# Fetching the rows of 5 of 416 table gathers on SyncE, row by row, in a DLRM interaction kernel on one Trainium2 core

## The reference

```python
e = stack([tbl_f[ids[:, f]] for f in range(26)], axis=1)        # (2048, 26, 64) float32 rows
x = layer_norm(dense @ Wd.T)                                     # (2048, 128)
y = layer_norm(einsum('bnd,ed->bne', e, Ws))                     # per row, 64 -> 128
y = layer_norm(einsum('bne,pn->bep', y, Wsi))                    # 26 rows mixed to 32
T = concatenate([x[:, None], swapaxes(y, 1, 2)], axis=1)         # (2048, 33, 128)
Z = einsum('bnd,bmd->bnm', T, T)[:, tril]                        # 528 products of pairs
z = layer_norm(Z @ Wl.T) * mask                                  # 512, 384 in use
h = relu(concat([z, dense]) @ W1 + b1); h = relu(h @ W2 + b2); out = h @ W3
```

## Time and profile before

| | |
|---|---|
| time, median of 3 runs | 577.3 us (575.38 to 578.61) |
| profiled execution, its own time | 577.42 us |
| its span, first to last instruction | 575.6 us |
| mean granted clock of TensorE | 0.976 |
| busy: PE / POOL / DVE / ACT | 505.9 / 400.8 / 397.2 / 293.6 us |
| first gather, start of the last one | 3.7 us, 528.7 us |

### The profile page before, as it was taken

How to read it: one execution, slowest core, us unless ns; L and a number is a source line. 1 busy time by engine, 2 the same in 40 slices (tenths; PEclk the granted TensorE clock), 3 DMA queues, 4 the chain that set the end, 5 groups by cost and what they waited for, 6 DMA issues and landing times.

```text
span 575.6 us, 18049 instructions
## 1 busy us (share of the span) xinstructions
PE 505.9 (88%) x7271; PEld 378.5 (66%) x7271; DVE 397.2 (69%) x707; ACT 293.6 (51%) x760; POOL 400.8 (70%) x422
## 2 busy tenths in 40 slices
PE   1969779999999898999989998988999899889975
PEld 1844457777776676777666766666676767668664
DVE  4787876777777767777676768766776777767800
ACT  1533565555554555545545646545454645555533
POOL 5777777777777777777777777777777777776000
PEclk9988799999999999899989999998999999999998
DMA  7711311313131312213131312213131211313020
GB/s 259 252 27 30 81 37 27 90 29 90 30 90 29 90 27 70 49 29 91 29 90 27 85 34 68 52 27 89 30 90 30 79 39 39 79 29 87 3 63 1
DMA packets 30999, 35.91 MB, mean 62 GB/s; under 512 B 10588, under 2 KB 19749, under 8 KB 30916
## 3 DMA queue, kind: packets, MB, share of 16 engines
q0 software_dynamic: 13408, 13.81, 12.5%
q1 hardware_dynamic: 17508, 20.94, 11.0%
HBM read 25.54 MB, written 9.18 MB: 60 GB/s over the span
## 4 chain that ended last, share of the span: by engine, by line
POOL 58%; issue 23%; PE 7%; DVE 5%; DMA 5%; ACT 2%; DVEq 0%; ACTq 0%
POOL rows L567 58%; DMA rows<-in_table,ids_based 5%; PE bank_z L700 2%; PE bank_z L633 1%; DVE scaled L397 1%; DVE scaled L372 1%; DVE y L407 1%; PE bank_aw L731 1%; DVE r_vec L433 1%; DVE bank_z L425 1%; ACT y_std L888 1%; PE bank_z L731 1%; PE bank_d L731 0%; DMA ids_based<-in_ids_based 0%; PE bank_z L681 0%
## 5 line engine op out<-in xcount | busy, mean ns | idle before, releaser
L567 POOL DMA_INDIRECT rows<-in_table,ids_based x416 | 399.4, 960 | 129.8 <-issue 122.0
L417 DVE TENSOR_REDUCE y_var<-y_sq 128x32 f32<-128x1024 f32 x63 | 76.9, 1220 | 41.3 <-ACT y_sq L882 41.1
L882 ACT ACTIVATE y_sq<-y 128x512 f32<-128x512 f32 x128 | 80.2, 631 | 34.2 <-DVE y L407 33.6
L433 DVE TENSOR_TENSOR r_vec<-y,bank_z 128x512 f32<-128x512 f32 x128 | 82.3, 684 | 2.4
L666 PE MATMUL bank_b<-mixed,gs_row 64*128 64x512 f32 x128 | 76.9, 682 | 7.8 <-ACT mixed L918 6.1
L681 PEld LDWEIGHTS bank_z<-r_vec 128*32 128x32 f32 x4096 | 46.0, 110 | 56.5 <-issue 54.7
L425 DVE RECIPROCAL bank_z<-y_std 128x32 f32<-128x32 f32 x63 | 22.8, 361 | 84.7 <-ACT y_std L888 84.7
L666 PE MATMUL bank_c<-mixed,gs_row 64*128 64x512 f32 x128 | 76.9, 682 | 0.0
L700 PE MATMUL bank_z<-wl,zd 128*128 128x512 f32 x160 | 75.2, 615 | 0.0
L639 PE MATMUL bank_z<-gram,rows_t 128*128 128x128 f32 x416 | 66.4, 300 | 8.7 <-ACT rows_t L903 8.7
L911 ACT ACTIVATE row_std<-row_var,eps 128x8 f32<-128x8 f32 (+1 forms) x64 | 19.2, 300 | 107.0 <-DVE row_var L381 97.7
(11 more groups left out here) (122 smaller groups left out, 633.8 us busy)
## 6 DMA issues: line engine op xcount, KB each, us to landing
zx<-zs SPq DMA_DIRECT2D x15, 560.0 KB, 3.6
rows<-in_table,ids_based POOLq DMA_INDIRECT x416
dense_t<-in_dense_t SPq DMA_DIRECT2D x1, 2048.0 KB, 9.1
wl<-in_wl SPq DMA_DIRECT2D x1, 1280.0 KB, 12.8
w<-in_w SPq DMA_DIRECT2D x1, 1280.0 KB
zd<-zx SPq DMA_DIRECT2D x15, 80.0 KB
zd<-zx SPq DMA_DIRECT2D x15, 70.0 KB
zd<-zx SPq DMA_DIRECT2D x16, 60.0 KB
```

Source lines behind the costliest of these rows:

```text
L417: v.tensor_reduce(y_var[:, k % BANKS, :], y_sq[:, k % 2, :, :].rearrange("e a (s p) -> e (a s) p", p=PROJ), AX_X, ALU.add).then_inc(y_var_ ...
L433: ins = v.tensor_tensor(r_vec[:, quad:quad + SPB // QUAD, :, Y0:PAD], y[:, k % 2, blk, :].rearrange("e (g s p) -> e g s p", g=SPB // QUAD, ...
L567: nc.gpsimd.indirect_dma_start(rows[t % 2][:, c, D * blk:D * (blk + 1)], None, io["table"], bass.IndirectOffsetOnAxis(ap=ids_all[:, n:n + ...
L882: nc.scalar.activation(y_sq[:, k % 2, blk, :], y[:, k % 2, blk, :], ACT.Square).then_inc(y_squared, 1)
```

## The change

Of the 26 gathers of tiles 3, 6, 9, 12 and 15 one is dropped, that of chunk 12, block 1, the last of its tile. Its 128 rows are fetched by SP with one DMA each, 640 in all. The row numbers lie in `own_ids`, on one partition: the ids and the first row of their table, which DVE adds up during the preparations. SP loads four row numbers at a time from there into registers, and issues four DMAs whose source address comes from them. It does 44 rows before its loop over the tiles, and then 44 in each turn of that loop: 4 between the store to `zx` and the wait for it, and 40 after the seven loads of `zd`. The buffer of rows is kept for four tiles in place of two, since SP writes to it long before POOL gets to that tile. POOL's wait on `rows_scaled` stays as it was.

```diff
+ROWS_KEPT = 4
+OWN_TILES = (3, 6, 9, 12, 15)
+OWN_CHUNK, OWN_BLK = CHUNKS - 1, 1
+OWN = P * len(OWN_TILES)
+OWN_FIRST, OWN_PART, OWN_BETWEEN = 44, 44, 4
+
+def gathers_of(t, q):
+    return [(c, blk) for c in GROUPS[q] for blk in range(2) if t not in OWN_TILES or (c, blk) != (OWN_CHUNK, OWN_BLK)]
...
-        rows = [sb(f"rows{i}", [P, CHUNKS, 2 * D]) for i in range(2)]
+        rows = [sb(f"rows{i}", [P, CHUNKS, 2 * D]) for i in range(ROWS_KEPT)]
+        own_ids = sb("own_ids", [1, 2, OWN], I32)
...
             add_row_base(1, TILES)
+            dve.wait_ge(s_own, 16)
+            v.tensor_tensor(own_ids[:, 1, :], own_ids[:, 1, :], own_ids[:, 0, :], ALU.add).then_inc(own_ready, 1)
...
             sp.dma_start(ids_based[:], io["ids_based"]).then_inc(s_ids, 16)
+            sp.dma_start(own_ids[:], io["own_ids"]).then_inc(s_own, 16)
...
+            def fetch(first, end):
+                end = min(end, OWN)
+                for at in range(first, end, 4):
+                    if at == 0:
+                        sp.wait_ge(own_ready, 1)
+                    if at % P == 0 and OWN_TILES[at // P] >= ROWS_KEPT:
+                        sp.wait_ge(rows_scaled, BANKS * (OWN_TILES[at // P] - ROWS_KEPT + 1))
+                    _, numbers = nc.values_load_multi_w_load_instructions(
+                        own_ids[0:1, 1, at:at + 4], engines=(mybir.EngineType.SP,), ...)
+                    for n in range(4):
+                        g, p = divmod(at + n, P)
+                        t = OWN_TILES[g]
+                        sp.dma_start(rows[t % ROWS_KEPT][p:p + 1, OWN_CHUNK, D * OWN_BLK:D * (OWN_BLK + 1)],
+                                     io["table"][bass.DynSlice(numbers[n], 1), :]).then_inc(own_landed[g], 16)
+
             sp.wait_ge(prep, prep_at["zd"])
+            fetch(0, OWN_FIRST)
             for t in range(TILES - 1):
                 sp.wait_ge(zs_kept, BANKS * (t + 1))
                 if t:
                     sp.wait_ge(z_moved, Z_MOVES * t)
                 sp.dma_start(zx.rearrange("j p k g i -> (j p) k g i"), zs[:]).then_inc(z_out, 16)
+                at = OWN_FIRST + OWN_PART * t
+                fetch(at, at + OWN_BETWEEN)
                 sp.wait_ge(z_out, Z_OUT * (t + 1))
                 if t:
                     sp.wait_ge(l_done, t)
                 for k in range(BLOCKS):
                     move_in(sp, k, z_moved)
+                fetch(at + OWN_BETWEEN, at + OWN_PART)
...
             def turn(k):
-                pe.wait_ge(gathered[t % 2][q], (t // 2 + 1) * (32 * len(GROUPS[q])))
+                pe.wait_ge(gathered[t % 2][q], 16 * sum(len(gathers_of(s, q)) for s in range(t % 2, t + 1, 2)))
+                if t in OWN_TILES and q == BANKS - 1:
+                    pe.wait_ge(own_landed[OWN_TILES.index(t)], 16 * P)
```

More of the change, by code:

```diff
@@ L177, in tower @@
         out_row = sb("out_row", [1, B])
+        s_own = sem("own_loaded")
         s_ids, s_small, s_wsi, s_wl, s_dense, s_top = (
@@ L183, in tower @@
         ids_ready = sem("ids_ready")
+        own_ready = sem("own_ready")
+        own_landed = [sem(f"own_landed_{t}") for t in OWN_TILES]
         prep = sem("prep")
@@ L372, in square_form @@
                 v.tensor_tensor(scaled[:, a:b, :], bank_g[:, 0:(b - a) * P].rearrange("p (c n) -> p c n", n=P),
-                                rows[t % 2][:, a:b, :], ALU.mult).then_inc(quad_done, 1)
+                                rows[t % ROWS_KEPT][:, a:b, :], ALU.mult).then_inc(quad_done, 1)
             def row_mean_square(k):
@@ L397, in scale_rows @@
                 v.tensor_tensor(scaled[:, a:b, :].rearrange("p c (a d) -> p (c a) d", d=D),
-                                rows[t % 2][:, a:b, :].rearrange("p c (a d) -> p (c a) d", d=D),
+                                rows[t % ROWS_KEPT][:, a:b, :].rearrange("p c (a d) -> p (c a) d", d=D),
                                 row_r[:, 2 * a:2 * b].rearrange("p (n o) -> p n o", o=1)
@@ L523, in _ @@
                 sp.dma_start(dst[:], io[src], max_dma_last_dim=PIECE).then_inc(s_top, 16)
+            def fetch(first, end):
[6 more added lines that the diff above has]
+                    _, numbers = nc.values_load_multi_w_load_instructions(
+                        own_ids[0:1, 1, at:at + 4], engines=(mybir.EngineType.SP,), min_val=0, max_val=io["table"].shape[0] - 1,
+                        skip_runtime_bounds_check_because="a row number of a table of that many rows, by the inputs' kind")
+                    for n in range(4):
[3 more added lines that the diff above has]
+                                     io["table"][bass.DynSlice(numbers[n], 1), :]).then_inc(own_landed[g], 16)
             sp.wait_ge(prep, prep_at["zd"])
+            fetch(0, OWN_FIRST)
             for t in range(TILES - 1):
@@ L563, in gather @@
                     pool.wait_ge(rows_scaled, k - 2 * BANKS + 1)
[L564 to L569, removed]
+                for c, blk in gathers_of(t, q):
+                    n = t * 2 * CHUNKS + 2 * c + blk
+                    nc.gpsimd.indirect_dma_start(
+                        rows[t % ROWS_KEPT][:, c, D * blk:D * (blk + 1)], None, io["table"],
+                        bass.IndirectOffsetOnAxis(ap=ids_all[:, n:n + 1], axis=0)).then_inc(gathered[t % 2][q], 16)
             for k in range(QUARTERS):
@@ L632, in turn @@
                 for n, c in enumerate(GROUPS[q]):
-                    mm = pe.transpose(bank_t[:, n * P:(n + 1) * P], rows[t % 2][:, c, :], ident[:])
+                    mm = pe.transpose(bank_t[:, n * P:(n + 1) * P], rows[t % ROWS_KEPT][:, c, :], ident[:])
                 mm.then_inc(turned, 1)
@@ L1100, in laid_out @@
     ids = ids.reshape(TILES, 2, 2, CHUNKS, HALF).transpose(2, 4, 0, 3, 1)
+    own = [2 * CHUNKS * t + 2 * OWN_CHUNK + OWN_BLK for t in OWN_TILES]
+    own_base = np.repeat(first_row[feature].T, 2, axis=1)[:, 2 * OWN_CHUNK + OWN_BLK]
+    own_ids = np.stack([np.tile(own_base, len(OWN_TILES)), ids.reshape(P, -1)[:, own].T.reshape(-1)])[None]
     wsi = np.asarray(x["L0_rec_Wsi"])
@@ L1150, in laid_out @@
                                     axis=1),
+        "own_ids": own_ids.astype(np.int32),
         "ident": np.eye(P, dtype=f32),
```

## The result

The changed kernel takes 574.0 us in the median of 13 runs (571.8 to 575.67), against 577.65 us for the kernel before in as many. The ratio is 0.9936, with a 95% interval of 0.9916 to 0.9956: 2.5 to 4.9 us are gained, 3.7 at the middle, where 5.0 was forecast.

What follows compares the result with a forecast made beforehand. The prediction took POOL's gathers, 1.25 us a step, as the bound. Four of five dropped gathers count, minus 5.0 us, with all added work at 0: 577.4 to 572.4, less 0.1 for the median, 572.3 us; range 570.2 to 581 us.

Steps and rivals of the forecast that it cites:

- the likeliest case: Whole kernel: the change gains 5.0 us, to 572.3 us; alone it spans 570.2 to 574 us, chance 0.56.
- The bound: POOL's gathers, one each 1.25 us, set the pace from beginning to end of POOL's work, though PE is 88% busy.
- some 25 us faster: PE from 197 to 517 us: without its 25.1 us of waits for gathered rows it could run about 8% faster.
- The fifth gather: Dropped gather for quarter 63, behind the last turn that waits (quarter 61): costs nothing and brings nothing.
- SP's price: SP's loop: four fetched rows at 0.37 us each plus 0.9 us for four registers, 2.4 us a group.
- The room of 26.3 us: SP's turn of 32.1 us less 3.2 and 2.6 us, left for ten groups of four rows, taken as 24 us.
- The point from which SP decides: SP's loop: above 2.67 us a group SP becomes the bound, with 5.5 us of slack over 13 turns; chance 0.22.
- The gathers beside the fetches: Shared DMA engines: the fetches stretch the gathers by 0, between bounds of 0 and 20 us.
- Rival B: Shared DMA engines: fetches stretch each of 411 gathers by 15 ns, which eats the gain; at half, 575.0 us; chance 0.12.
- The start: Preparations: DVE starts at about 6.4 us, and PE's 0.5 us of delay disappears in waits before or at 197 us.
- Does PE take over all 5.0 us?: PE up to quarter 61: waits suffice to take over four dropped gathers of 1.25 us each, so minus 5.0 us.
- Rival C: PE takes over only a part, as its clock falls more often with shorter pauses: half the gain, 574.8 us; chance 0.06.

Runs made afterwards that it cites:

- four_own: Changed kernel, but tile 15 is gathered whole again, so only tiles 3, 6, 9 and 12 lose a gather: 573.5 us, ratio 0.9928 to the kernel before.
- both416: Changed kernel, but POOL does all 416 gathers and SP also fetches the 640 rows, into a spare tensor: 578.8 us, ratio 1.0018 to the kernel before.
- both_again: Second run with all 416 gathers on POOL and the 640 rows fetched by SP into a spare tensor: 579.9 us, ratio 1.0030 to the kernel before.
- after: Profiled execution of the changed kernel itself: 572.97 us, span 571.2 us; median of its 13 runs 574.0 us.
- after_again: The changed kernel measured once more, unaltered: 574.0 us, ratio 0.9937 to the kernel before.
- block5: Changed kernel with five plain DMAs of 128 table rows (other data) in place of the 640 single-row DMAs: 574.6 us, ratio 0.9938 to the kernel before.
- late_ids: Changed kernel with the row numbers' load behind SP's seven small loads and DVE's addition after its first preparations: 574.0 us, ratio 0.9937 to the kernel before.
- all16: Changed kernel, but every tile's last gather is dropped, 16 plain DMAs of 128 table rows (other data) instead: 560.1 us, ratio 0.9704 to the kernel before.

## Why the prediction was right

The time lies in the range and the sign is right, by the likeliest case, though at the edge of its 570.2 to 574 us. Its steps, one by one.

**The bound.** POOL's pace, not PE's 88%: shown. Sixteen gathers less gave 17 us less, with the same work on PE. What was wrong is PE's distance: "some 25 us faster" from 197 to 517 us took its busy time for its pace. At 31.1 us a tile it had 17 us to give, so a gain of 25 us was never there; for five gathers it makes no difference.

**The fifth gather.** It "brings nothing": four_own agrees within its interval. The turn I named as the last that waits, quarter 61, moved to 58; both lie behind four dropped gathers, so the count stayed.

**SP's price.** A group was taken at 2.4 us, between 1.2 and 5.2, and measured 2.29. The two terms were each further off than their sum: a row was taken at 0.37 us and took 0.43, the four registers at 0.9 and took 0.57, so +0.24 and -0.33 us nearly cancel, which is luck. The room of 26.3 us for ten groups stood against 23, and SP's 2.8 us of waiting in a turn lie within the forecast 1 to 8. The 0.9 us was my choice between 0.05 and 2.5 us, and neither a row nor a run shows the round trip given as its reason: what the trace shows is a TENSOR_LOAD on SP's queue of 467 to 722 ns, 556 in the median. The low end of the pitch forecast, 2.1 us a group, had no row behind it either. The point from which SP decides, 2.67 us a group, wasn't varied by itself, but its sum of lateness minus 5.5 us of slack forecast two overloads within 4 us (591 for 594.8) and 6 us (651 for 645.6).

**The gathers beside the fetches.** Taken at 0: both416 and both_again have their last gather at 528.3 and 530.0 us, 528.7 in the kernel before. Rival B's 15 ns a gather would put it 6 us later, and is out.

**The start.** DVE's addition took 0.81 us and its preparations began at 6.23 us, for the 6.4 forecast. But PE came to quarter 8 at 90.94 us, 3.4 us later and not 0.5, and in this trace it didn't wait at quarter 22 (before at 196.99), where the first 1.25 us were to be taken; its first wait for rows behind the start is at quarter 33, 284.78 us. So PE's backlog lasted 88 us longer than the prediction had it, and its waits fell to 13.3 us and not "by some 4" from 25.1. It was gone well before quarter 58, so no cost of it can be seen in the end.

**The size.** The term that was off is the answer to "Does PE take over all 5.0 us?": minus 5.0 forecast, minus 3.7 measured (2.5 to 4.9). In the profiled execution the gather that quarter 58 waits for starts 487.99 - 483.64 = 4.35 us earlier, not 5.0: of those ahead of it 21 came over 1.3 us after the one before, and 16 in the kernel before. Quarter 61 is 4.8 us earlier and the end 4.4. In the kernel before, 1.75 us of waits (0.22, 0.45 and 1.08 at quarters 59 to 61) lay behind the pause at quarter 58, a cushion for anything that slows PE there. After the change this cushion is gone or smaller, and in four of the seven traces in the table below PE's clock fell to 0.50 behind that pause: from quarter 58 to 59 PE took 7.89 us in the changed kernel and 6.40 before. In both_again the same stretch took 9.06 us, with these matmuls behind a pause of 2.02 us:

```profile
493.47 0.55 PE L672 MATMUL bank_z<-ident,rows 128*128 128x128 f32 x3 [2.02 <-DMA rows<-in_table,ids_based]
493.94 1.83 PE L693 MATMUL bank_aw<-wsi_b,scaled 64*128 64x64 f32 x16
495.70 1.65 PE L678 MATMUL bank_z<-gram,rows_t 128*128 128x128 f32 x6
```

The granted clock of these stretches, in the changed kernel behind its pause and in the kernel before over all of its last part (columns as above):

```profile
489.40:492.80 3.40, 3.40 (x16) 2.08 (x14) 2.75 (x5) 1.20 (x3) 2.49 (x4) 0.50 0.21 44
```
```profile
400.00:565.00 165.00, 148.30 (x2154) 111.03 (x2152) 107.87 (x190) 85.28 (x218) 99.80 (x105) 1.00 0.20 50
```

The other traces agree. Against the trace of the kernel before, where quarter 58 also began behind a pause (2.06 us) but no fall followed:

| trace | gather for quarter 58 earlier by | end earlier by | at the lower clock behind quarter 58 |
|---|---|---|---|
| after | 4.35 us | 4.4 us | 3.4 us |
| after_again | 6.65 us | 5.6 us | 3.4 us |
| block5 | 2.89 us | 1.8 us | 6.8 us |
| both_again | -1.29 us | -3.6 us | 6.8 us |
| late_ids | 5.42 us | 6.5 us | none |
| four_own | 4.98 us | 5.0 us | none |
| both416 | 0.28 us | 0.3 us | none |

Without a fall PE takes over all of POOL's shift, with one it loses some 1, 1 and 2 us in three of four. The four falls came behind pauses of 2.0 to 2.3 us; in the other three traces a pause of 1.8 to 2.1 us and its fall lay a tile earlier, at 455 to 467 us, with waits for rows still behind it. This is rival C in a form I had not written: not more falls of the clock, but a fall that nothing behind it absorbs. Rival C as written is not borne out: the mean granted clock is 0.974 over the executions of after_again and 0.971 over those of the kernel before on the same chip, and all16, with hardly a pause for rows, has 0.984 against 0.970. That the lost cushion makes up the 1.3 us of the medians is only argued, since the kernel before has one trace. The 1.4 us of both416 and both_again, where no gather is dropped, speak for a further cost that stays open; a kernel with nothing but the four buffers, the load and the addition was not run.

## What to carry to other kernels

Before work is taken off the bounding queue, find the last point at which anyone waits for it: only what is removed ahead of it counts. Then ask for the next engine's own pace in a stretch where it doesn't wait for that queue, not from its busy share (31.0 us a tile here, where busy time said 29.8); the trace before the change may have such a stretch. An idle queue is a place for the work only up to its period: price one item with everything around it, multiply, and compare with the period, since two groups too many turned -0.6% into +2.9%.

## What the runs showed of the hardware

A gather that started together with a store of 560 KB landed later than one that started well ahead of it. In the chain of the changed kernel, with these stores at 321.54, 385.96, 419.17 and 483.67 us (start, us from start to landing):

```profile
306.51 2.46 DMA rows<-in_table,ids_based
385.92 3.54 DMA rows<-in_table,ids_based
404.14 2.40 DMA rows<-in_table,ids_based
419.12 3.87 DMA rows<-in_table,ids_based
```

With the gather of 483.64 us and its 4.40 us these are 3.5 to 4.4 us beside a store and 2.4 to 2.5 us at 15 us ahead of one. The store isn't all, as gathers 7 to 8 us away from one took 3.28 us (360.95, behind SP's seven loads) and 3.10 (513.70 in the kernel before). Since the store follows the last copy to `zs`, and quarter 58 (like the third quarter of other tiles) needs the gather that starts then, PE's longest waits for rows lie there, 2.29 us in the last case. Small DMAs, 640 of 256 bytes, did nothing of the kind: the gather of 404.14 us runs amid the fetches and landed after 2.40 us, and those of 374.58, 440.46 and 472.99 us in the kernel before, without fetches, after 2.37, 2.45 and 2.44.

A row of 256 bytes that SP fetches by an address from a register took 0.43 us from one to the next. That is more than one of the seven loads of `zd`, which carry up to 80 KB (2.61 / 7 = 0.37 us).

Registers loaded eight at a time took 782 ns in the median against 556 for four, so 57 ns for each further register.
